# Making each scatter of an attention turn wait for a place in TensorE's score pairs

## What is computed

```python
h = _layernorm(x) * (1 + ca) + sa
x = x + ga * attention(h)            # 16 heads of 8, RoPE, causal softmax, projection
h = _layernorm(x) * (1 + cb) + sb
probs = sigmoid(h @ router_w.T + expert_bias)
top_w, top_idx = top_k(probs, 8)     # top_w is divided by its sum and multiplied by 2.5
routed = sum over the 8 experts of top_w * (silu(h @ w_gate[e].T) @ w_down[e].T)
x = x + gb * (routed + silu(h @ w_gate_shared.T) @ w_down_shared.T)
```

## Time and profile before

| What | Value |
|---|---|
| median of three runs | 2200.42 us |
| the profiled execution, its own time | 2189.18 us |
| its span in the trace | 2187.3 us |
| attention: first product of turn -1 to first expert load | 49.76 to 1366.39 us |
| a steady turn | about 75.9 us |
| busy: PE (TensorE) | 1379.2 us, 63% |
| busy: DVE (VectorE) | 1190.1 us, 54% |
| busy: ACT (ScalarE) | 757.6 us, 35% |
| busy: POOL (GpSimd) | 1147.3 us, 52% |

### The profile page before, as it was taken

How to read it: one execution, slowest core, us unless ns; L and a number is a source line. 1 busy time by engine, 2 the same in 40 slices (tenths; PEclk the granted TensorE clock), 3 DMA queues, 4 the chain that set the end, 5 groups by cost and what they waited for, 6 DMA issues and landing times.

```text
span 2187.3 us, 33316 instructions
## 1 busy us (share of the span) xinstructions
PE 1379.2 (63%) x10342; PEld 692.4 (32%) x10342; DVE 1190.1 (54%) x4186; ACT 757.6 (35%) x1599; POOL 1147.3 (52%) x1190
## 2 busy tenths in 40 slices
PE   3568887877787787778778743877776777600000
PEld 1123333323332332333333311555454555400000
DVE  3657766677677676666767436433333333434333
ACT  0045444434444443344345411222544544400000
POOL 1101255555555554555465666001777777777776
PEclk9579778777877787777778856888878877755555
DMA  4594445454444445444444313999999999812211
GB/s 137 174 292 133 138 133 146 127 174 127 134 144 137 134 140 155 135 133 139 138 134 128 105 64 96 293 301 297 351 330 321 344 327 327 290 57 59 60 57 54
DMA packets 291644, 380.99 MB, mean 174 GB/s; under 512 B 46457, under 2 KB 175627, under 8 KB 291340
## 3 DMA queue, kind: packets, MB, share of 16 engines
q1 hardware_dynamic: 234508, 267.65, 40.7%
q0 software_dynamic: 32768, 67.17, 9.9%
q10 hardware_dynamic: 24192, 44.05, 5.4%
HBM read 218.52 MB, written 160.18 MB: 173 GB/s over the span
## 4 chain that ended last, share of the span: by engine, by line
PE 25%; POOL 21%; DVE 19%; DMA 12%; issue 10%; SPq 10%; ACT 2%; POOLq 0%; DVEq 0%; ACTq 0%
POOL vh L1392 17%; DVE masked L554 7%; SPq L1286 4%; PE bank L544 4%; DMA prob<-pages 4%; PE bank L693 4%; DMA km<-k_stacks 4%; SPq L479 3%; PE bank L424 3%; POOL pages L769 2%; DMA k_stacks<-k_part 2%; PE bank L630 2%; PE bank L868 2%; PE bank L490 1%; DMA pages<-h,pos_s 1%
## 5 line engine op out<-in xcount | busy, mean ns | idle before, releaser
L1392 POOL DMA_INDIRECT vh<-results,pos_all x512 | 506.1, 988 | 316.0 <-DMA results<-v_ext 161.3
L554 DVE CUSTOM_DVE_ANT_0 masked<-bank,cb_all 128x512 bf16<-128x512 f32 (+3 forms) x1024 | 444.6, 485 | 280.2 <-PE bank L544 277.9
L769 POOL DMA_INDIRECT pages<-h,pos_s x512 | 504.8, 986 | 165.0 <-issue 164.6
L657 ACT ACTIVATE prob<-bank 128x512 f32<-128x512 f32 x640 | 347.5, 597 | 410.7 <-PE bank L642 406.4
L544 PE MATMUL bank<-km,qm 64*128 64x512 bf16 (+3 forms) x1024 | 210.4, 361 | 171.3 <-DVE rmax L554 106.7
L1402 DVE TENSOR_TENSOR vh<-vh,wts_all 128x1024 f32<-128x1024 f32 x64 | 79.2, 1238 | 406.1 <-DMA vh<-results,pos_all 406.1
L693 PE MATMUL bank<-prob,v_ext 128*32 128x512 f32 (+3 forms) x2048 | 234.2, 539 | 2.0 <-ACT prob L657 2.0
L1310 PE MATMUL bank<-c_all,prob 128*128 128x128 f32 x672 | 135.1, 334 | 148.9 <-DMA prob<-pages 148.0
L630 PE MATMUL bank<-qe,ke 64*128 64x512 bf16 (+3 forms) x1024 | 161.1, 346 | 36.5 <-ACT prob L657 33.0
L544 PEld LDWEIGHTS bank<-km,qm 64*128 64x128 bf16 x1024 | 50.3, 99 | 333.3 <-DVE rmax L554 194.6
L1310 PEld LDWEIGHTS bank<-c_all,prob 128*128 128x128 f32 x672 | 86.7, 165 | 192.0 <-DMA prob<-pages 179.3
(11 more groups left out here) (187 smaller groups left out, 1850.8 us busy)
## 6 DMA issues: line engine op xcount, KB each, us to landing
prob<-wexp SPq DMA_DIRECT2D x672, 96.0 KB
pages<-free_rows SPq DMA_DIRECT2D x42, 1024.0 KB, 7.5
prob<-pages SPq DMA_DIRECT2D x168, 256.0 KB
results<-v_ext ACTq DMA_DIRECT2D x168, 256.0 KB
qm<-q_stacks SPq DMA_DIRECT2D x64, 256.0 KB, 3.4
km<-k_stacks SPq DMA_DIRECT2D x64, 256.0 KB, 4.7
qe<-q_stacks SPq DMA_DIRECT2D x64, 256.0 KB, 3.8
ke<-k_stacks SPq DMA_DIRECT2D x64, 256.0 KB, 4.5
```

The source lines that it names most:

```text
L554: last = e.tensor_tensor_reduce(out=masked[:, g % 2, c0:c0 + (i + 1) * P], in0=MX[g % 2][:, c0:c0 + (i + 1) * P], in1=mask_w[:, S - (i + 1 ...
L657: e.activation(prob[:, slot, :], ST[g % 3][:, :], ACT.Exp, scale=SCALE).then_inc(s_exa, 1)
L769: e.indirect_dma_start(out=pages, in_=h2[:, t, :], in_offset=None, out_offset=bass.IndirectOffsetOnAxis(ap=pos_s[:, t * TOPK + k:t * TOPK ...
L1392: e.indirect_dma_start(out=y8[:, i, k, :], out_offset=None, in_=results[0:ready * 4 * GRP * P, :], in_offset=bass.IndirectOffsetOnAxis(ap= ...
```

## The change

A new function `paced` wraps the list of scatters. For each it works out the place within the turn, turns the place into a pair of TensorE's sequence (the one before that place), and makes GpSimd wait for the end of that pair before it issues the scatter: a pair of maxima (`s_mxp`) or of exponentials (`s_exp`); in the last turns, where there are no maxima, always a pair of exponentials. The two streams of scatters of a turn are paced, except in turn 16; the second half of a sequence is now placed from 0.0 to 0.4 of the turn (0.44 before), the first half from 0.52 to 0.98 (0.54 to 0.99 before).

```diff
+        def paced(steps, i, start, end):
+
+            def step(e, f, at):
+                pairs, part = divmod(int(4 * UNITS * at) - 2, 2)
+                if pairs >= 0 and (part == 1 or i + 1 >= NB):
+                    wait(e, s_exp, 4 * UNITS * i - UNITS + 2 * (pairs + 1))
+                elif pairs >= 0:
+                    e.wait_ge(s_mxp, 4 * UNITS * (i + 1) + 2 * (pairs + 1))
+                f(e)
+            share = (end - start) / len(steps)
+            return [{"pool": lambda e, f=st["pool"], at=start + share * (k + 0.5): step(e, f, at)}
+                    for k, st in enumerate(steps)], start, end
...
-            if 3 <= i <= NB:
+            if 3 <= i < NB:
+                streams.append(paced(scatters(i - 3)[SHARE:], i, 0.0, 0.4))
+            if i == NB:
                 streams.append((scatters(i - 3)[SHARE:], 0.0, 0.44))
             if 2 <= i < NB:
-                streams.append((scatters(i - 2)[:SHARE], 0.54, 0.99))
+                streams.append(paced(scatters(i - 2)[:SHARE], i, 0.52, 0.98))
```

## The result

| | before | after |
|---|---|---|
| median (7 runs each) | 2200.08 us | 2185.05 us |
| lowest to highest | 2191.42 to 2208.45 | 2182.18 to 2188.31 |
| ratio, 95% interval | | 0.9938 [0.9915, 0.9961] |
| the profiled execution | 2189.18 us | 2188.23 us |

The change takes 15 us, 0.6%. The forecast was 2185.7 us. The two profiled executions do not show this gain as a whole: that of before is 10.9 us under its median, that of after 3.2 us above its own.

What follows compares the result with a forecast made beforehand. In steady turns one scatter, held behind the q part on in-order GpSimd, delayed `h` and then TensorE; in the tail GpSimd was the bound. -14.4 - 2.4 + 2.1 = -14.7 us took 2200.42 to 2185.7 us, range 2168 to 2203.

Steps and rivals of the forecast that it cites:

- The last scatter of a sequence: Turns 3 to 13: issued ahead of the q part, the 32nd scatter no longer delays ScalarE's `h`; -14.4 us.
- the bounds of 11.1 and 17.6: Limits in us on removing `h`'s wait: turn 2 against the mean of turns 3 to 13, and TensorE's idle time.
- TensorE's clock takes it back: Rival, chance 0.22: the lead at L811 is lost by the k part in each turn, leaving -0.3 us, 2200.1 us.
- the prediction's own signs of being wrong: Among them: turns 3 to 13 have a mean granted clock of 0.74 or less and last as long as before.
- the clock adds: Rival, chance 0.10: the 2.42 us lead at L811 is kept, 26.6 us in eleven turns, 2173.5 us in all.
- Scatters at the handoff: Behind the k part: seven scatters instead of nine speed the load of km, 0.2 us in 12 handoffs, -2.4 us.
- The other gates of a steady turn: Steady turns: the remaining waits on pairs fit within the slack of the q and k parts; no cost.
- The price of a wait that is already met: GpSimd's scatters: each met wait costs 0.05 us; 0.4 us inside the k part's slack, 0.7 in the tail.
- the rival built on it: Chance 0.13: met waits cost more and delay the k part; at 0.5 us each, 2222 us; slower from 0.31.
- Turns 14 to 16: Tail, bound by GpSimd: held-back scatters end 1.4 us later and thirteen waits add 0.7, a cost of 2.1 us.
- The gates do nothing: Rival with no chance of its own: the order alone moves the last scatter, with the same gain.
- The sum: All terms over the whole kernel: -14.4 - 2.4 + 2.1 = -14.7 us, from the median 2200.42 to 2185.7 us.

## Why the prediction was right

The time, 2185.05 us against 2185.7, its sign and its mechanism came out as forecast. The whole change gave -15.0 us here and -13.4 and -14.6 in the two later series. That the size is so near is in part luck, as the sum at the end of this section shows. By its steps:

**The last scatter of a sequence (-14.4 us forecast).** Right in mechanism: the wait of `h` in turns 3 to 13 is gone, the scatter stands ahead of the q part at 25 us, and with the old places and all gates (where the scatter is behind the q part again) the gain is gone. The size, measured as the mean over ten profiles, is 12.0 us, inside the bounds of 11.1 and 17.6 and near the lower one, though all of TensorE's 17.6 us behind `h` went. Turn 2 of before, from which that bound came, was the better guide than the middle: steady turns of after do what turn 2 did, with L811 at 41.0 us and the k part at 62.0 in the mean.

**TensorE's clock takes it back (0.22).** Half true. Turn 8 shows the full form: 2.42 us of lead at L811, nothing left at the k part, at 0.65 instead of 0.82. Over the eleven turns 2.42 x 11 = 26.6 us were to be had and 12.0 stayed. So the clock did not cancel the gain, but took back more than half of what the lead at L811 promised. Of the prediction's own signs of being wrong, one half came (a clock of 0.74 or less in turns 3 to 13: it was 0.73) and the other did not (that they last as long as before). The other rival, that the clock adds, is false. The Trainium skill's page "TensorE: Matmul & The Clock Gate", section "What's actually happening", says that the throttled state is the default and activity releases it. I had drawn from it that less idle time can only raise the clock, and these windows do not agree with that: TensorE's wait behind `h` went, and the granted clock of turns 3 to 13 went from 0.77 to 0.73 in the first pair of profiles. It is 0.76 in the second profile with old places and 0.73 to 0.75 in all eight with new ones.

**Scatters at the handoff (-2.4 us forecast).** Wrong. Seven scatters follow the k part instead of nine, as said, but from the k part to the next first product it is 12.93 us before and 12.92 after in the mean of turns 3 to 13. The step took one load of km with no scatters about it, 0.46 us quicker, for an effect of two of them. TensorE's idle time ahead of L544 did get less (51.2 us against 60.0), but the handoff is no shorter for it: TensorE arrives later there.

**The other gates of a steady turn (0).** Right: the k part has 3.98 us of slack, and turns 3 to 13 take as long without gates.

**The price of a wait that is already met (0.7 us forecast), and the rival built on it (0.13).** Wrong, and the rival false: a burst with gates keeps its spacing. In the burst behind the k part of turn 8, shown above, every scatter has a wait that is already met, and they follow each other at 0.30 us. Here are scatters of turn 15 of after. The one at 1194.98 was released by a pair of scores just ahead of it and still follows at 0.30 us; those at 1193.72 and 1234.84 were held up:

```profile
1193.72 0.95 POOL L769 DMA_INDIRECT pages<-h,pos_s  x1 [2.95 <-PE bank L642]
1194.98 0.95 POOL L769 DMA_INDIRECT pages<-h,pos_s  x1 [0.30 <-PE bank L642]
1196.23 0.96 POOL L769 DMA_INDIRECT pages<-h,pos_s  x1 [0.30 <-issue]
...
1231.27 0.96 POOL L769 DMA_INDIRECT pages<-h,pos_s  x1 [0.30 <-issue]
1234.84 1.18 POOL L769 DMA_INDIRECT pages<-h,pos_s  x1 [2.62 <-PE bank L642]
...
1257.78 0.95 POOL L769 DMA_INDIRECT pages<-h,pos_s  x1 [0.30 <-issue]
```

The 0.46 us at the first scatter of a sequence, from which I worked out 0.05 us a wait, is not a price of waits like these; what it is was not tried.

**Turns 14 to 16 (+2.1 us forecast).** Right in kind, but only a half to two thirds of what was measured. The gate of pair 17 is the row at 1234.84: 3.57 us behind its predecessor instead of 1.26, so 2.3 us late where the step said 2.2. In turn 15 `h` waits 0.80 us; the step said 0.7. Between `h` of turn 15 and `h` of turn 16 the loss is 1.0 us (50.31 against 49.28), close to what the step had. What it missed lies ahead of that: GpSimd is held up in turn 14 (3.85 us at 1126.63, 2.88 at 1147.89) and at the start of turn 15 (3.63 at 1189.82, 2.95 at 1193.72) as well, where before the scatters went out 1.26 us apart. The prediction's sign, `h` of turn 16 coming 1 to 2 us later relative to turn 14, was not met: it comes 134.37 us after the start of turn 14 against 127.72, 6.65 us later (3.6 and 3.2 in the two other profiles of the whole change). The removal of the gates in these turns gave 3.1 us (2182.72 to 2179.66), the profiles say some 4. In the first pair of profiles it is 5.7, of which 2.6 is there already at `h` of turn 14, which comes 25.58 us into the turn against 22.94. The granted clock there is 0.74 in the first 64 us of after and 0.82 in the first 59 of before, so a part of the 5.7 may well be the clock's.

**The gates do nothing (no chance of its own).** By the time this could not be told from the forecast, as I wrote, and at the 2200 us level it is what happened: the places do it all, and by the medians the gates cost between 1 and 6 us, which the intervals do not tell from nothing. I should have weighed it as more than a footnote. At the 2578 us level it is wrong the other way round: there the gates are worth 4% (in one kernel, of one series) and the places nothing.

**The sum.** By the profiles it would be 12.0 gained instead of 14.4, nothing at the handoff instead of 2.4, and 3 to 4 lost at the end instead of 2.1: -8 to -9 us. All three errors go the same way, and yet the medians say -13.4 to -15. So some 5 us of the gain come from elsewhere, and the forecast hit the time only with them. Most of it stands in a stretch that the change does not touch: from the first page load to the end it is 821.0 and 824.1 us in the two profiles with old places and 815.9 to 822.3 (mean 818.5) in the eight with new ones. That is 4 us, but the two ranges overlap and nothing here says why it should be so. It stays open.

## What to carry to other kernels

Look for the one instruction that an in-order engine holds back behind a step it does not depend on, while the engine is idle: moving it past that step was worth 0.75 to 0.9% at the 2200 us level, and needed no wait at all. A stretch of the same program that already lacks the wait (turn 2 here) was a better measure of what its removal brings than the idle time behind it, since it includes what the clock takes back. Waits that only pace a burst showed no cost when met, but they sit on the path where the paced engine is the bound (the last turns): leave them out there, and measure the change without them as well before they are kept. Here that would have dropped them at the 2200 us level and kept them at the 2578 us level.

## What the runs showed that I had not expected

- The same kernel took 2200 us in two series and in the first comparison, and 2578 us in another. In that one ScalarE stood idle for 202 us of the steady part and for 464 us of the experts' phase with nothing in the trace that ended it, and only in the phases in which GpSimd issues indirect DMAs. The experts' phase, 821 us otherwise, took 1030 (2564.6 - 1534.15).
- There, pacing the scatters gave 0.9584 [0.9557, 0.9611], an effect seven times that of the whole change elsewhere, and the order alone 1.0017. A ratio from one series did not carry over to another.
- A semaphore wait on GpSimd that is already met has no price that shows: scatters stay 0.30 us apart with and without one.
- With the wait of `h` gone the granted clock of turn 8 rose between `h` and L811 (0.63 to 0.85) and fell from L811 to the k part (0.82 to 0.65). Over turns 3 to 13 TensorE was busy for 24.8 us more with the same products, and more than half of the lead at L811 was gone at the k part.
